# The count matrix of a four-layer graph kernel: free banks by way of GpSimd, clears in pairs, one heavy cell a lane

## The reference

```
x += mean over incoming edges of (h[src] @ W + b)                        # layer 0
x += layernorm(h + update(h, sum of gated messages(h[src], edge_attr)))  # layer 1
x += relu(h @ Ws.T + bs + (sum of filter(edge_attr) * h[src]) @ Wn.T + bn)  # layer 2
h  = relu(h @ W_in.T + b_in)                                             # layer 3
for l in range(3): h = h + relu(sum over edges of norm * (h @ W[l].T)[src] + b[l])
x += h @ W_out.T + b_out
```

## Time and profile before

| | |
|---|---|
| median of three runs | 8681.88 us (8679.63 to 8687.66) |
| the profiled execution | 8686.3 us, its span 8684.5 us |
| TensorE busy, share of the span | 5822.4 us, 67% |
| VectorE | 4301.2 us, 50% |
| ScalarE | 1758.3 us, 20% |
| GpSimd | 3273.6 us, 38% |
| counting stage, first to last matmul | 777.7 to 1558.4 us |
| first pass by the count matrix | from 1621.7 us |
| the three convolutions | from 7669.7 us to the end |

### The profile page before, as it was taken

How to read it: one execution, slowest core, us unless ns; L and a number is a source line. 1 busy time by engine, 2 the same in 40 slices (tenths; PEclk the granted TensorE clock), 3 DMA queues, 4 the chain that set the end, 5 groups by cost and what they waited for, 6 DMA issues and landing times. The chain is left out here.

```text
span 8684.5 us, 135899 instructions
## 1 busy us (share of the span) xinstructions
PE 5822.4 (67%) x29812; PEld 4117.1 (47%) x29813; DVE 4301.2 (50%) x14700; ACT 1758.3 (20%) x3520; POOL 3273.6 (38%) x3354
## 2 busy tenths in 40 slices
PE   4313666794555554555454778888878888889999
PEld 4312443573333333333332455555555555677877
DVE  7877777424666666666666233333333333432222
ACT  0013888202111111111112111111111111110000
POOL 0105000004555555555552555555555555300000
PEclk9856777897777777777777566556665656689999
DMA  1231332553333333333332222222222222256666
GB/s 31 102 100 61 107 103 100 187 221 75 71 72 70 71 69 71 71 70 71 71 69 31 43 34 34 35 34 35 35 34 34 35 35 35 23 207 246 255 240 232
DMA packets 1052581, 764.66 MB, mean 88 GB/s; under 512 B 868977, under 2 KB 978241, under 8 KB 1032914
## 3 DMA queue, kind: packets, MB, share of 16 engines
q1 hardware_dynamic: 664738, 483.03, 18.4%
q0 software_dynamic: 131808, 243.11, 11.8%
q10 hardware_dynamic: 255904, 37.09, 2.5%
HBM read 657.77 MB, written 143.22 MB: 92 GB/s over the span
## 5 line engine op out<-in xcount | busy, mean ns | idle before, releaser
L1874 POOL DMA_INDIRECT rows<-node_rows,idx_ring x1612 | 1528.9, 948 | 1201.8 <-DMA idx_ring<-src_all 707.7
L1874 POOL DMA_INDIRECT rows<-node_rows_wide,idx_ring x1612 | 1545.9, 959 | 1099.9 <-DMA idx_ring<-sorted_pairs 574.3
L1923 PE MATMUL ps_sum<-hots,act_ring 128*97 128x128 f32 x3224 | 647.2, 365 | 1281.2 <-DVE hots L1908 530.2
L1911 DVE TENSOR_SCALAR hots<-iota,lane_all 128x128 f32<-128x128 f32 x1612 | 462.9, 288 | 1807.3 <-remote 1250.0
L1923 PEld LDWEIGHTS ps_sum<-hots,act_ring 128*97 128x97 f32 x3224 | 545.9, 230 | 1579.0 <-DVE accT L1917 1107.3
L1923 PE MATMUL ps_sum<-hots,msg 128*96 128x128 f32 x3224 | 722.6, 399 | 397.6 <-DVE hots L1911 194.1
L1386 PE MATMUL ps_conv<-conv_rows,adj_ring 128*128 128x288 bf16 x7497 | 942.5, 288 | 44.3 <-DVE conv_rows L1345 22.0
L1917 DVE TENSOR_TENSOR accT<-accT,ps_sum 97x128 f32 (+1 forms) x3224 | 908.3, 282 | 49.3 <-issue 16.7
L1386 PEld LDWEIGHTS ps_conv<-conv_rows,adj_ring 128*128 128x128 f16 x7497 | 738.3, 99 | 233.3 <-issue 23.1
L2031 PEld LDWEIGHTS ps_w<-w2w,hid 97*128 97x128 f32 x3224 | 581.8, 271 | 530.8 <-issue 475.5
L1950 PE MATMUL ps_e<-w1e,aT 128*128 128x384 f32 x1612 | 817.9, 644 | 18.0 <-DVE aT L1986 15.5
(11 more groups left out here) (341 smaller groups left out, 6088.8 us busy)
## 6 DMA issues: line engine op xcount, KB each, us to landing
adj_ring<-adjacency SPq DMA_DIRECT2D x144, 2176.0 KB, 7.8
adjacency<-panels SPq DMA_DIRECT2D x588, 128.0 KB, 1.7
idx_ring<-sorted_pairs SPq DMA_DIRECT2D x1612, 1.0 KB
attr_ring<-sorted_attr ACTq DMA_DIRECT2D x1612, 16.0 KB
rows<-node_rows_wide,idx_ring POOLq DMA_INDIRECT x1612
attr_ring<-sorted_attr SPq DMA_DIRECT2D x1612, 8.5 KB
rows<-node_rows,idx_ring POOLq DMA_INDIRECT x1612
sorted_attr<-in_edge_attr SPq DMA_DIRECT2D x5, 5000.0 KB
```

The source lines that it names most:

```text
L1874: g.indirect_dma_start(out=rows[:, r, j, 0:width], out_offset=None, in_=table, in_offset=bass.IndirectOffsetOnAxis(ap=idx, axis=0)).then_i ...
L1911: last = v.tensor_scalar(hots[:, r % 2, j, :], iota[:, :], lane, None, ALU.is_equal)
L1923: last = pe.matmul(ps_sum[0:M, r % 2, j, :], what(r, j), hots[:, r % 2, j, :], start=True, stop=True)
```

## The change

- **Free banks.** VectorE no longer loads panel numbers or waits for banks; it waits only for its own ring of one-hots. GpSimd loads the panel numbers of 16 tiles (`free`), and for every 4 of them (`GATE`) waits on `emptied` for the last one's panel and adds one to a new semaphore, `bank_free`. TensorE waits for `bank_free` before every fourth tile.
- **Clears.** ScalarE clears two banks in one instruction of 1024 columns, after the copy of every even panel.
- **Heavy cells.** One a lane: the key in the middle of the sorted lane. All keys of the lane equal to it are counted and taken out, however few they are. So `SB` = 50. The rows of heavy cells are now written by VectorE, right after `take_heavy`; GpSimd only stores them.
- **Chunks.** `NC` = 5 chunks of ten source blocks. In a convolution the weights now follow one pair after chunk 1 has begun; for the first panel of a layer both steps stand a chunk later.
- **Counts of any size.** The count of a heavy cell was 1024 or nothing, now it can be any number up to 2048; it goes into the rows of layer 0 as two bf16 columns, which are added (290 columns instead of 289).

```diff
-HALF = GK // 2
+GATE = 4
...
-HEAVY = 1024
-HV = SN // HEAVY
+MIDDLE = SN // 2
+HV = 1
 SB = NB + HV
-NC = 3
+NC = 5
...
@@ def take_heavy(v, cur)
+                    middle, bits = keys[cur][:, MIDDLE:MIDDLE + 1], keys_i[cur][:, MIDDLE:MIDDLE + 1]
+                    same, count = keys[1 - cur], run_f[:, 2, :]
...
+                    link(v, v.tensor_scalar(same, keys[cur], run_f[:, 1, :], None, ALU.is_equal, ALU.add, accum_out=count))
+                    step(v, v.tensor_tensor(keys[cur], keys[cur], same, ALU.max))
+                    sorted_in.append((sorted_step.n, cur))
...
-                    for k in range(HV):
-                        step(v, v.tensor_scalar(runs[:, k, :], runs[:, k, :], other[:, k:k + 1], same[:, k:k + 1],
-                                                ALU.mult, ALU.add))
...
+                    for k in range(NK):
+                        cols = PANEL_COLS[k]
+                        last = v.tensor_scalar(heavy_cell[:, 2 * k * WD:2 * k * WD + cols], target[:, 0:cols],
+                                               float(2 * k * WD), heavy_to[:, 0:1], ALU.add, ALU.is_equal)
+                    last.then_inc(heavy_cells.sem, 1)
@@ block "adjacency", VectorE
-                            if n * HK % HALF == 0:
-                                empty = v.value_load(part_panel[:, dyn(q * GK + n * HK + HALF - 1, 1)], min_val=1,
-                                                     max_val=PANELS + 1)
-                                past(v, block_mm, (q - HB) * GK + n * HK + HALF)
-                                v.sem_inc(passed_v.sem, 1)
-                                v.wait_ge(emptied.sem, empty)
+                            past(v, block_mm, (q - HB) * GK + (n + 1) * HK)
@@ TensorE
+                            if j % GATE == 0:
+                                past(pe, bank_free, q * (GK // GATE) + j // GATE + 1)
@@ ScalarE
-                    none = zeros[:, 0:1].to_broadcast([P, 2 * WD])
+                    none = zeros[:, 0:1].to_broadcast([P, 4 * WD])
...
-                            if k > 0 or later:
+                            if (place * NK + k) % 2 == 0 and (k > 0 or later):
+                                old = (place * NK + k - 2) % BANKS * 2 * WD
                                 a.wait_ge(panel_kept.sem, i * NK + k)
-                                a.activation(ps_b[:, old:old + 2 * WD], none, ACT.Copy).then_inc(emptied.sem, 1)
+                                a.activation(ps_b[:, old:old + 4 * WD], none, ACT.Copy).then_inc(emptied.sem, 2)
@@ GpSimd
-                    g.iota(target[:, :], [[1, 2 * WD]], base=0, channel_multiplier=0,
-                           allow_small_or_imprecise_dtypes=True).then_inc(made.sem, 1)
-                    g.wait_ge(made.sem, MADE + ADJ_MADE + 1)
-                    for k in range(NK):
-                        for n in range(HV):
-                            last = g.tensor_scalar(heavy_cell[:, k, n, 0:PANEL_COLS[k]], target[:, 0:PANEL_COLS[k]],
-                                                   heavy_to[:, n:n + 1], float(-2 * WD * k), ALU.subtract, ALU.is_equal)
-                        last.then_inc(heavy_cells.sem, 1)
...
+                    def free(q, turn, r):
+
+                        panel = nc.values_load_multi_w_load_instructions(
+                            part_panel[:, dyn(q * GK, GK)], [POOL], min_val=1, max_val=PANELS + 1)[1]
+                        for j in range(0, GK, GATE):
+                            g.wait_ge(emptied.sem, panel[j + GATE - 1])
+                            g.sem_inc(bank_free.sem, 1)
+                    turns(g, [(free, 0)], Q2, HB)
@@ def mean_layer
-                    multiply_panels(pe, ring, nodes, 3 * D + 1, ps, 0, (0, 0, 1), lambda k, c, pair: None)
+                    multiply_panels(pe, ring, nodes, 3 * D + 2, ps, 0, (0,) * (NC - 1) + (1,), lambda k, c, pair: None)
...
-                            counts = ps[:, 2 * pair:2 * pair + n, 3 * D]
-                            link(v.tensor_scalar(dinv[:, b], counts, 1.0, None, ALU.add))
-                            link(v.tensor_scalar(edges[:, 0:n], counts, 1.0, None, ALU.max))
+                            link(v.reduce_sum(edges[:, 0:n], ps[:, 2 * pair:2 * pair + n, 3 * D:3 * D + 2], AX.X))
+                            link(v.tensor_scalar(dinv[:, b], edges[:, 0:n], 1.0, None, ALU.add))
+                            link(v.tensor_scalar(edges[:, 0:n], edges[:, 0:n], 1.0, None, ALU.max))
@@ def graph_layers, TensorE
-                            turn_at, weigh_at = ((0, 0), (0, 1)) if not isinstance(k, int) or k < NK - 1 else ((0, 0), (1, 0))
+                            turn_at, weigh_at = ((0, 0), (1, 0))
+                            if isinstance(k, int) and k == 0:
+                                turn_at, weigh_at = ((1, 0), (2, 0))
```

More of the change, by code:

```diff
@@ L624, in graph_kernel @@
             panel_end = accT[64:65, 0:PANELS].bitcast(I32)
+            heavy_cell = ends_k[:, :, :].rearrange("p a b -> p (a b)").bitcast(F16)
+            target = tmp("target", [P, 2 * WD], F16)
             lanes = tmp("lanes", [P, TP // 2, ENDS, 2], BF16)
@@ L912, in take_heavy @@
                 def take_heavy(v, cur):
[L914 to L919, removed]
+                    middle, bits = keys[cur][:, MIDDLE:MIDDLE + 1], keys_i[cur][:, MIDDLE:MIDDLE + 1]
+                    same, count = keys[1 - cur], run_f[:, 2, :]
+                    real = run_f[:, 0, :]
+                    step(v, v.tensor_copy(run_f[:, 1, :], middle))
+                    step(v, v.tensor_scalar(real, middle, 1.0, None, ALU.is_lt))
                     step(v, v.tensor_scalar(run_i[:, 0, :], bits, 13, (NB_BITS - 1) * P, ALU.logical_shift_right,
@@ L1166, in take @@
                             bank = (place * NK + k) % BANKS * 2 * WD
-                            old = (place * NK + k - 1) % BANKS * 2 * WD
                             if not isinstance(i, int):
@@ L1282, in keep_turned, with norm_relu @@
                          ACT.Copy).then_inc(turned_kept.sem, 1)
-        def norm_relu(table, turned_to=None, ones=(), clear=True, squares=None, centred_already=False):
+        def norm_relu(table, turned_to=None, ones=(), zeroed=None, clear=True, squares=None, centred_already=False):
             with ExitStack() as ctx:
@@ L1309, in _ @@
                         g.memset(t, 1.0).then_inc(made.sem, 1)
+                    if zeroed is not None:
+                        g.memset(zeroed, 0.0).then_inc(made.sem, 1)
                     if clear and ones:
@@ L1313, in _ @@
                         g.memset(accT[:, :], 0.0).then_inc(made.sem, 1)
-                made.n += len(ones) + (1 if clear else 0)
+                made.n += len(ones) + (1 if clear else 0) + (0 if zeroed is None else 1)
                 if table:
@@ L1639, in _ @@
                         split = split0 + layer * (NK + 1)
-                        need = (0, 0, split + 1) if layer == 0 else (split - NK + 5, split - NK + 9, split + 1)
+                        need = (0,) * (NC - 1) + (split + 1,)
+                        if layer:
+                            need = tuple(split - NK + 1 + (CB * (c + 1) - 1) // 4 for c in range(NC - 1)) + (split + 1,)
                         def after(k, c, pair):
-                            turn_at, weigh_at = ((0, 0), (0, 1)) if not isinstance(k, int) or k < NK - 1 else ((0, 0), (1, 0))
+                            turn_at, weigh_at = ((0, 0), (1, 0))
+                            if isinstance(k, int) and k == 0:
+                                turn_at, weigh_at = ((1, 0), (2, 0))
                             if isinstance(k, int) and k == 0:
```

34 lines of the change are left out of this document (17 added, 17 removed).

## The result

| | before | after |
|---|---|---|
| median | 8684.77 us (4 runs, 8679.63 to 8711.24) | 8869.25 us (4 runs, 8835.01 to 8878.24) |
| ratio, 95% interval | | 1.0199 (1.0165 to 1.0233) |
| the profiled execution | 8686.3 us | 8878.2 us |
| counting stage, first to last matmul | 777.7 to 1558.4 | 788.8 to 1746.2 |
| first pass by the count matrix | 312.9 us | 305.7 us |

The kernel is slower by 2.0%, and the forecast of 8865 us is 4 us from the median. Up to the end of the counting stage the changed kernel loses 187.8 us; the multiplications give back 7.2 and 16.3; and an edge pass that nobody touched is 27.2 longer.

A forecast was written before the change was run, and what follows sets the result against it. The prediction took ScalarE's issue to bound the counting stage before and GpSimd's sequencer after, at 5.55 us a batch. 196 + 1 - 15 = +182 on 8686.3 gave 8868, set at 8865 us; range 8780 to 8950.

The forecast's parts named there:

- The bound: Counting stage: the pace passes from ScalarE's own issue to GpSimd's sequencer, 175 batches at 5.55 us, 971 us.
- The batch: GpSimd, per 16 tiles in the counting stage: checks 3.58, load 1.28, semaphores, address and loop 0.7; 5.55 us, no overlap.
- The two rivals on the load: GpSimd's load: short, 0.50 us, total near 8730, chance 0.07; long, behind VectorE's one-hots, near 9060, chance 0.06.
- The stage's end: Counting stage ends near 1755 us instead of 1559, +196; GpSimd's stores first, 7.2; keys stored about 1 us later.
- The multiplications: Four passes by the count matrix: -24 + 1 + 19 - 11 = -15 us, between -35 and +5.
- The handover: Convolutions: chunks of ten shorten TensorE's cover while VectorE finishes a pair; 6.3 us lost a layer, 19 in three.
- wait between layers: TensorE between convolution layers: first chunk's wait -3.1 us, heavy row -1.3 and -2.3 with gather 2 later; twice, -11.
- ScalarE's 14.2 us a block with pairs: Counting stage: paired clears save about 1.7 us a block, some 82 us in all, if other engines keep up.
- three gaps in ScalarE's block: Counting stage before: 1.29, 1.87 and 1.68 us in place of 0.52, from panel-end loads and checks, mostly not TensorE waits.
- first rival: Counting stage: GpSimd's batch below about 3.98 us, ScalarE decides, the 82 us are gained; near 8590, chance 0.05.
- The sum: Whole kernel: 196 + 1 - 15 = +182 us on the profiled execution's 8686.3.

The follow-up runs named there:

- no_relay: Changed kernel without GpSimd's grants: VectorE again loads panel numbers and waits for cleared banks; 7331.3 us, ratio 0.9960 to the kernel before.
- both_max: Changed kernel with a register maximum replacing range checks on GpSimd (4 waited values a batch) and ScalarE (13 panel ends a block); 7283.5 us, 0.9886.
- pool_checks_4: Changed kernel, but GpSimd range-checks only the 4 of 16 loaded panel numbers that it waits on; 7301.6 us, ratio 0.9921 to the kernel before.
- repeated run: The changed kernel itself, unaltered, run again on a chip where the kernel before takes 7368.3 us; 7532.5 us, ratio 1.0227.
- no_relay_one_load: Against the kernel without relay, with single clears, ScalarE's maximum and later turn (7255.1 us): ScalarE's 13 panel ends in one load, not three; 7297.2 us.

## Why the prediction was right

**The bound.** GpSimd's sequencer, with its checks, sets the stage's pace: shown, by the bursts of 16, by the distance of the loads with 16 and 12 checks, and by no_relay.

**The batch.** 5.55 forecast, 5.497 measured, and its terms can be read one by one. GpSimd's sequencer over one batch of the changed kernel, 1197.45 to 1201.25 us:

```profile
L1193 POOLq FUSED_REGOPS  x16: 147/147/152, 1197.6 to 1201.0; - x16
L1193 POOLq SEQ_ASSERT  x16: 18/18/18, 1197.7 to 1201.1; - x16
```

A check starts 0.227 us after the one before it. Averaged over the batches of the stage, the 16 checks take 3.64 us, for 3.58 in the forecast; the load 1.12 (1.055 at the median) for 1.28, less than TensorE's for as many values; and the semaphores, the address and the loop 0.74, for 0.7. So only the load was sized wrong, by 0.16, and the other two hid 0.10 of it. The two rivals on the load fall: it is neither GpSimd's own 0.50 nor a wait behind the one-hots. The Trainium skill's floor of about 600 ns for a tensor_load (DMA: Bandwidth & Descriptors, Latency and other measured facts) holds here for 16 values, but not for ScalarE's loads of four, which go down to 305 ns (both_max).

**The stage's end.** +187.8 for +196: the batch, times 175, is the difference. The stores took 6.98 for 7.2. The keys came 3.1 us later instead of 1; what is lost ahead of the sort stood in no term.

**The multiplications.** -23.5 in the two traces for -15. TensorE's waits for fresh rows at the turns, before (7669 to 8680 us) and after (7877 to 8870 us); the numbers are us in all, times, longest:

```profile
PE ps_curT L1622 <- DVE fresh L1724: 2.0, 3, 0.7
PE ps_curT L1628 <- DVE fresh L1734: 21.4, 36, 1.6
```

The handover was well sized, 19.4 us more for 19. The wait between layers was mis-sized, by about 9 us for two: the heavy row comes 5.8 and 7.8 us sooner, where I allowed 2.3, apart from the first chunk's 3.1, which did go.

**An error that did not show.** The step that fell is ScalarE's 14.2 us a block with pairs, 82 us gained if the other engines keep up. Alone the pairs gain nothing; behind a relay with 4 checks the block is 15.2. The forecast called the three gaps in ScalarE's block mostly no waits for TensorE. Its own rows say otherwise: two of the three end at TensorE, 0.67 and 1.06 us, and one, 1.25, at ScalarE's issue. The waits of the kernel before from 800 to 1500 us, and TensorE's group from 770 to 1565:

```profile
ACT panels L1172 <- PE ps_blocks L1148: 92.7, 91, 4.0
ACT panels L1172 <- issue: 34.8, 32, 3.9
...
L1148 PE MATMUL ps_blocks<-end_hot 128*128 128x256 bf16 x2800 | 490.2, 337 | 290.8 <-DVE end_hot L1126 205.2 <-issue 83.3
```

ScalarE waits for TensorE, TensorE for VectorE, and VectorE for both the earlier trace rows. The stage before ran close to such a ring: without ScalarE's checks it gains 1.4 us a block and then stops. With that the first rival ("GpSimd keeps up") was priced too well: -58 us in pool_checks_4 where I had -96. The forecast stood because GpSimd's 5.5 us a batch, 19.5 a block, hid all of it. This part of it was luck.

**A coincidence.** The sum was 182 and the spans differ by 191.8, but 27.2 of that are the untouched pass; the change's own terms come to 187.8 - 7.2 - 16.3 = 164. So the 4 us between forecast and median are luck too; without the 27 the median would be some 23 us under the forecast, still in its range. The repeated run, where that pass is not longer, shows 7532.5 - 7368.3 = +164 us as well: the change costs 164, on the low side of the forecast's range.

## What to carry to other kernels

A wait on a register that comes from memory has a price on the sequencer that no busy share shows: count the range checks (here 0.23 us for each loaded value) and check only the values that are waited for, or take a maximum (33 to 38 ns), which keeps the lower bound and gives up the upper one. Before a wait is moved from one engine to another, add up what the new engine issues per unit of work and set it against the pace of the stage. And where three engines wait for one another in a ring, a gain on one is worth what an experiment shows, not what its row says.

## What the hardware showed beside it

The price of a load into registers depends on more than the number of values. ScalarE's load of 13 values took 1.24 us in the first block, then 1.08 to 1.11 in every fourth (at 841.16, 900.92 and 962.86 us in no_relay_one_load) and 2.8 to 3.07 in the others; GpSimd's load of 16 takes 1.05. A block's 13 values begin at a multiple of four only in every fourth block, and GpSimd's 16 always do. The kernels with three loads a block say the same. In their twelve traces, ScalarE's loads of four values that begin at a multiple of four take 0.31 to 0.54 us, all 312 of them. The other 864 take 0.90 us or more, 0.98 at the median. For five values it is 0.54 to 0.77 against 1.1 us or more. So one long load replaced three long ones at no gain. No run moved the table, so that the beginning itself is the reason, and not something else that returns every fourth block, was not tested; a table with 16 places a block would test it.

The other surprise is the 1.3 ms between the first executions and the experiments. It lies in the two edge passes (2667 and 2728 us against 2038 and 2017 for the changed kernel). SyncE's index loads in the pass of layer 1, first in the first trace of the changed kernel, then in the repeated run:

```profile
L1859 SPq FUSED_REGOPS  x1612: 3/37/1406, 2190.9 to 4850.5; - x180
L1859 SPq MOVE idx_ring<-sorted_pairs x1612: 3/29/1394, 2191.0 to 4850.6; - x180
...
  POOL rows L1884: 639.1, 176
```

```profile
L1859 SPq FUSED_REGOPS  x1612: 37/37/47, 2189.9 to 4211.1; - x180
L1859 SPq MOVE idx_ring<-sorted_pairs x1612: 29/29/37, 2190.0 to 4211.2; - x180
...
  POOL rows L1884: 91.7, 266
```

The same register move takes 29 ns at the median in both, but up to 1.39 us in the first, and GpSimd waited 639 us there for the indices against 92. In the first trace of the kernel before it waited 606.5 us: of the 32 us more in the changed kernel, 27 are found again in its longer edge pass. On SyncE and ScalarE together, 1344 register instructions take more than 0.6 us in the first trace of the kernel before and 1357 in that of the changed one, some 950 us in all, none of them in the counting stage; the twelve traces of the experiments have not one. What stalls them was not found.
